# A two-block graph network: beta of the first norm added by ScalarE to the turned tokens

## The reference, cut to what matters

```python
h = jnp.maximum(_layernorm(x, axis=-1), 0.0)
x = x + _L0_gnn_ref(h, adj, ...)      # 8 heads of masked attention, relu
h = jnp.maximum(_layernorm(x, axis=-1), 0.0)
x = x + _L1_gnn_ref(h, adj, ...)      # below
# in _L1_gnn_ref, for each of 3 layers l:
    scores = si[:, :, None] + sj[:, None, :] + attn_b[l]     # then leaky relu, mask
    attn = jax.nn.softmax(scores, axis=-1)
    agg = jnp.einsum('bij,bjd->bid', attn, x)
    h = layernorm(x + agg, g1[l], beta1[l])
    ff = jax.nn.gelu(h @ W1[l] + b1[l], approximate=False) @ W2[l] + b2[l]
    x = layernorm(h + ff, g2[l], beta2[l])
```

## Time and profile before

| | us |
|---|---|
| median of 3 runs | 1536.05 |
| range of the runs | 1535.99 to 1536.13 |
| the profiled execution | 1535.7 |
| its span, first to last instruction | 1533.5 |
| one slot of the second block, most | 25.1 to 25.2 |
| TensorE busy | 1490.6 |
| VectorE busy | 1390.3 |
| ScalarE busy | 1102.2 |
| GpSimd busy | 898.8 |

### The profile page before, as it was taken

One profiled execution on the slowest core, in us unless ns is written; L12 is line 12 of the kernel. 1 busy time (PEld: TensorE's weight loads), 2 busy tenths in 40 slices (PEclk: granted clock), 3 DMA queues, 4 the chain that ended last, 5 costly groups with the idle time before them and its releaser, 6 DMA issues. The chain is left out here.

```text
span 1533.5 us, 35213 instructions
## 1 busy us (share of the span) xinstructions
PE 1490.6 (97%) x11360; PEld 1272.8 (83%) x11360; DVE 1390.3 (91%) x4315; ACT 1102.2 (72%) x1948; POOL 898.8 (59%) x1006
## 2 busy tenths in 40 slices
PE   5899999899999999999999999999999999999997
PEld 3677777778888888888989888988888888888887
DVE  7999999879999999999898999898999998989864
ACT  5788888267777767677777676777777677777774
POOL 5799998336463647463636465645455655455565
PEclk9999999599999999999999999999999999999999
DMA  6643334500000102110001121100011211000001
GB/s 199 167 136 124 134 124 132 169 21 15 8 15 10 47 25 87 35 42 8 15 24 33 38 74 42 36 8 15 25 32 40 71 49 29 8 15 8 15 29 55
DMA packets 70890, 82.79 MB, mean 54 GB/s; under 512 B 29280, under 2 KB 54112, under 8 KB 70752
## 3 DMA queue, kind: packets, MB, share of 16 engines
q1 hardware_dynamic: 69120, 74.76, 16.9%
q0 software_dynamic: 816, 3.15, 0.7%
q10 hardware_dynamic: 816, 3.15, 0.5%
HBM read 38.95 MB, written 25.17 MB: 42 GB/s over the span
## 5 line engine op out<-in xcount | busy, mean ns | idle before, releaser
L874 ACT ACTIVATE bank<-bank,b_col 128x512 f32<-128x512 f32 x384 | 252.0, 656 | 282.9 <-PE bank L773 281.7
L797 PE MATMUL bank<-w_hi,hid_hi 128*128 128x256 f32 x1528 | 433.9, 284 | 6.7 <-DVE hid_lo L1057 6.7
L797 PE MATMUL bank<-w_lo,hid_hi 128*128 128x256 f32 x1528 | 431.8, 283 | 0.0
L797 PE MATMUL bank<-w_hi,hid_lo 128*128 128x256 f32 x1528 | 431.8, 283 | 0.0
L1057 DVE TENSOR_TENSOR hid_lo<-bank,hid_hi 128x512 fp32r<-128x512 f32 x384 | 262.2, 684 | 66.6 <-ACT hid_hi L879 65.3
L773 PE MATMUL bank<-nT_hi,w_hi 128*128 128x512 f32 x768 | 317.3, 413 | 1.2 <-DVE nT_lo L1186 1.2
L797 PEld LDWEIGHTS bank<-w_hi,hid_hi 128*128 128x128 f32 x1528 | 291.2, 191 | 22.9 <-DVE hid_lo L1057 9.7
L773 PE MATMUL bank<-nT_lo,w_hi 128*128 128x512 f32 x768 | 303.4, 395 | 0.0
L773 PE MATMUL bank<-nT_hi,w_lo 128*128 128x512 f32 x768 | 301.9, 393 | 0.0
L797 PEld LDWEIGHTS bank<-w_lo,hid_hi 128*128 128x128 f32 x1528 | 291.5, 191 | 11.8
L797 PEld LDWEIGHTS bank<-w_hi,hid_lo 128*128 128x128 f32 x1528 | 291.4, 191 | 0.0
(11 more groups left out here) (144 smaller groups left out, 3124.5 us busy)
## 6 DMA issues: line engine op xcount, KB each, us to landing
raw_weights<-xin SPq DMA_DIRECT2D x96, 128.0 KB, 2.3
xin<-in_x_dram SPq DMA_DIRECT2D x16, 512.0 KB, 4.0
first_block_out<-x_res SPq DMA_DIRECT2D x16, 512.0 KB, 2.7
second_block_in<-x_act SPq DMA_DIRECT2D x16, 512.0 KB, 3.7
xin<-second_block_in SPq DMA_DIRECT2D x16, 512.0 KB, 3.9
x_fin<-first_block_out SPq DMA_DIRECT2D x16, 512.0 KB, 4.1
out_dram<-x_fin SPq DMA_DIRECT2D x15, 512.0 KB, 2.9
xh_other<-xh SPq DMA_DIRECT2D x128, 33.0 KB, 1.9
```

Of the source, the lines that this page charges most:

```text
L797: mm = pe.matmul(FF[t // 2][:, (t % 2) * D:(t % 2 + 1) * D], a[:, r, t * P:(t + 1) * P], w[:, l, c, :], start=(c == 0 and t % 2 == 0 and p ...
L874: act.activation(h[:], h[:], ACT.Gelu, bias=b1_col[:, l, c:c + 1]).then_inc(s_gelu, 1)
```

## The change

- b1_col is loaded as it is; the splits of beta1, the 96 products and the two additions go. beta1_col stays for the whole kernel.
- ScalarE's `split_n` takes two passes for each half of the tokens: Identity with scale g1 and bias beta1, in place in NT_B, and a rounding copy to nT_hi. The first half is made at chunk 5, the second at chunk 6.
- VectorE's nT_lo is a plain subtraction; its first half comes between low(5) and low(6), its second behind low(7).
- `hidden(0)` waits for each half where it uses it.
- At the start of the second block exp(1,1) comes ahead of gelu(0), VectorE makes scores(0,1) before and dots_of(0,2) behind the first split, TensorE does spread(1,1) ahead of turn_n(0,0), and the first slot has turn_attn and aggregate where the others have them.
- ScalarE's queue issues the loads of W1 at step 3 instead of 2.

```diff
@@ first block, ScalarE
-                    if isinstance(tau, int) and tau == 2:
+                    if isinstance(tau, int) and tau == 3:
                         act.wait_ge(q_ld, 64)
                         for l in range(L):
                             act.dma_start(raw[:, l]...
@@ first block, VectorE
-                    if isinstance(tau, int) and tau == HEAD - 1:
-                        dve.wait_ge(s_col, 48)
-                        dve.tensor_copy(beta1_parts[:, :, :, 0], beta1_col[:]).then_inc(s_beta, 1)
-                        dve.wait_ge(s_beta, 1)
-                        dve.tensor_tensor(beta1_parts[:, :, :, 1], beta1_col[:], beta1_parts[:, :, :, 0].bitcast(F32),
-                                          ALU.subtract).then_inc(s_beta, 1)
@@ TensorE
                 def hidden(U, s, c):
                     l, g = layer_group(s)
-                    if c == 0:
-                        pe.wait_ge(s_nlo, KD * (U + 1))
                     at_least(pe, s_split, CF * U + c - 2)
                     for k in range(KD):
+                        if c == 0:
+                            pe.wait_ge(s_nlo, KD * U + k + 1)
@@
-                def bias(l, cs):
...
                 def tail(tau):
-                    if tau == NT + 5:
-                        bias(0, range(CF))
                     if tau == NT + 6:
                         pe.wait_ge(s_samer, 1)
                         pe.wait_ge(q_ev, NT)
                         spread(0, 0)
-                        bias(1, range(CF // 2))
-                    if tau == NT + 7:
-                        bias(1, range(CF // 2, CF))
                     if tau == NT + 8:
                         turn_attn(0, 0)
                     if tau == NT + 9:
                         pe.wait_ge(q_vh, 2 * NT)
                         aggregate(0, 0)
-                        bias(2, range(CF))
                 def before():
+                    spread(1, 1)
                     turn_n(0, 0)
-                    spread(1, 1)
@@ (in some)
-                            if nxt and c == (1 if U == 0 else 0):
+                            if nxt and c == 0:
                                 turn_attn(U + 1, s + 1)
-                            if nxt and c == (2 if U == 0 else 1):
+                            if nxt and c == 1:
                                 aggregate(U + 1, s + 1)
@@ ScalarE
-                def split_n(V, s):
+                def split_n(V, s, ks=range(KD)):
                     l, g = layer_group(s)
-                    for k in range(KD):
+                    for k in ks:
                         act.wait_ge(s_nT, KD * V + k + 1)
-                        act.activation(nT_hi[:, s % 2, k, :], NT_B[k][:], ACT.Copy, scale=g1_col[:, l, k:k + 1]).then_inc(s_nhi, 1)
+                        act.activation(NT_B[k][:], NT_B[k][:], ACT.Identity, bias=beta1_col[:, l, k:k + 1],
+                                       scale=g1_col[:, l, k:k + 1]).then_inc(s_nfull, 1)
+                        act.wait_ge(s_nfull, KD * V + k + 1)
+                        act.copy(nT_hi[:, s % 2, k, :], NT_B[k][:]).then_inc(s_nhi, 1)
@@ (before)
                     split_n(0, 0)
-                    act.wait_ge(s_b1, 2)
+                    exp(1, 1)
@@ (in some)
-                            if nxt and c == (1 if U == 0 else 0):
+                            if nxt and c == 0:
                                 keep_attn(U + 1, s + 1)
                             high(U, s, c)
-                            if U == 0 and c == 0:
-                                exp(1, 1)
...
-                            if nxt and c == 5:
-                                split_n(U + 1, s + 1)
+                            if nxt and c in (5, 6):
+                                split_n(U + 1, s + 1, (c - 5,))
@@ VectorE (split_n)
                         dve.wait_ge(s_nhi, KD * V + k + 1)
-                        dve.scalar_tensor_tensor(nT_lo[:, s % 2, k, :], NT_B[k][:], g1_col[:, l, k:k + 1],
-                                                 nT_hi[:, s % 2, k, :].bitcast(F32), ALU.mult, ALU.subtract).then_inc(s_nlo, 1)
+                        dve.tensor_tensor(nT_lo[:, s % 2, k, :], NT_B[k][:], nT_hi[:, s % 2, k, :].bitcast(F32),
+                                          ALU.subtract).then_inc(s_nlo, 1)
@@ (before)
-                    dots_of(0, 2, range(0, 2))
-                    dve.wait_ge(s_bias, L)
...
+                    scores(0, 1)
                     first_part_over(dve)
                     split_n(0, 0)
-                    scores(0, 1)
+                    dots_of(0, 2, range(0, 2))
@@ (in some)
                         low(U, s, 5)
                         if nxt:
-                            split_n(U + 1, s + 1)
+                            split_n(U + 1, s + 1, (0,))
                         low(U, s, 6)
                         if nxt3:
                             dots_of(i, s + 3, range(0, 1))
                         low(U, s, 7)
+                        if nxt:
+                            split_n(U + 1, s + 1, (1,))
```

32 lines of the change are left out of this document (6 added, 26 removed).

## The result

The changed kernel takes 1514.56 us (median of 4 runs, 1514.12 to 1515.4), the kernel before 1536.02 us in the same set: ratio 0.9861, 95% interval 0.9844 to 0.9878, faster by 1.4%. Executions of the kernel before fall in two groups, 1533.3 to 1535.0 and 1536.2 to 1536.7 us in the set that has most of them, and the four of this set lie near the upper one. The profiled execution took 1515.0 us, its span 1513.2 us, 20.3 us less than before.

What follows compares the result with a forecast made beforehand. TensorE, busy for 97% of the span, bounds the kernel, VectorE the slots with a mask. 1.4 + 0.7 + 7.0 + 6.3 = 15.4 us off 1535.7 gives 1520.3, with 0.35 for the median 1520.6; range 1515 to 1527.5.

Steps and rivals of the forecast that it cites:

- first block: Before the second block: W1 loads issued a step later win 1.4 us, the split of beta leaving VectorE 0.7.
- hand-over: Start of second block: fewer bias products, earlier hidden(0), two table loads gone; 7.9 us less 0.9 given back, 7.0.
- mask slots: The 12 slots where VectorE also makes a mask: low(7) starts 1.2 us earlier, 6.3 us won of 7.5 lost.
- So in 35 slots nothing changes.: Second-block slots without a mask: VectorE's moved half only lengthens idle time or is covered, so no gain.
- I take 1.4: First block: hT(0) and hrelu(1) run before the W1 loads; VectorE 1.9 us earlier, then 1.6; bounds 0.3 and 1.9.
- The 0.7 for the split of beta: First block, step 15: VectorE's two instructions, 0.37 and 0.53 us less overlap, go; bounds 0.3 and 0.9.
- the three waits: VectorE's waits for TensorE before the first norm_n, 1.12, 1.25 and 1.61 us, behind bias products: 3.6 us won.
- the 0.9 that a held mask was to give back: Hand-over: make_mask(0,2) meets GpSimd's first base and is held, about 0.9 us lost.
- VectorE as the bound of the mask slots: Rival, chance 0.20: the dot products stay held in the 12 slots, 3.2 us or less won; 1523.8 to 1527.
- The clock rival: Rival, chance 0.10: hand-over gives 5 us or less, as the clock stays low or mask and base collide; 1522.6 to 1526.
- The slower rival: Rival, chance 0.04: ScalarE's new pass late for gelu(7) in 47 slots; 0.33 us beyond 0.9 covered eats the gain.
- The signs: Profile after: hid_lo waits gone but slot 0, first hidden matmul some 6 us earlier, hidden(3) some 9, src_hi at 14.8.

Runs made afterwards that it cites:

- the order alone: The kernel before with only VectorE's second nT_lo moved behind low(7) and TensorE waiting for each half by itself: 1525.57 us, ratio 0.9932.
- the extra wait: The changed kernel with one more, long fulfilled wait on ScalarE between exp(1,1) and the first gelu: 1514.05 us.
- the run with 128 bytes: The changed kernel with 128 bytes a partition left free behind beta1_col: 1509.05 us in a single execution, beside 1536.40 of the kernel before.
- the run with two more copies: The changed kernel with the rounding copy of the second nT_hi done three times, the visit 1.24 us longer: 1535.3 us, ratio 0.9999.

## Why the prediction was right or wrong

| part | forecast | bounds | found (us of the span, one trace of each kernel) |
|---|---|---|---|
| first block | 2.1 | 0.6 to 2.8 | 0.2 |
| hand-over | 7.0 | 5.2 to 8.4 | 7.0 |
| mask slots | 6.3 | 3.2 to 7.5 | 8.2 |
| other slots | 0 | none | 2.2 |
| places of the tiles | not seen | none | 2.8 |
| sum | 15.4 | | 20.4, measured 20.3 |

**The step that failed** is "So in 35 slots nothing changes." It rested on an empty list of waits. The starts of turn_n, 25.12 and 25.24 us apart by turns, said that something was lost in every second slot, and hid_lo(7) at 740.80 beside output(7) at 740.85 said where. The run with the order alone gives 2.2 us for these slots. The same oversight set the upper bound of the mask slots: 7.5 us is the loss against an ordinary stretch, taken as TensorE's own pace of 25.2 us a slot, and that pace had losses of its own. Against 25.12 the loss is 8.2, and all of it was won. The term of the mask slots is a right mechanism of a wrong size, 6.3 for 8.2: low(7) came 1.07 us earlier (forecast 1.2), and the dot products in front of it stayed held, 1.39 us.

**The places** are a gain of 2.8 us that no row of before could tell, and no part of what the change is about. The time lies 0.44 us below the range, so each of the two unforeseen gains, this one and the 2.2 us of the ordinary slots, was enough to put it there: with the tiles at their old places the changed kernel takes 1517.09 us, inside the range. Shown is that 64 bytes of padding take it back; why TensorE's matmuls of 256 columns take 280 instead of 282 ns with one place and not with another stays open.

**The first block** was over-sized. By the table over eighteen traces the two steps together are worth 0.8 us, for 2.1, within the bounds of 0.6 to 2.8; the pair in the table above has 0.2. "I take 1.4" held for some us: the lead is 1.7 at VectorE's first src_hi and 1.1 at the third no_edge. The forecast let TensorE do its part at the pace of the trace of before, but with the work moved forward, in the changed kernel's trace though not in all, more of it falls in the slow time: the score products took 0.78, 0.63 and 0.58 us where they had taken 0.49, 0.38 and 0.38. The 0.7 for the split of beta was not found: in that pair VectorE's lead is 0.1 us more behind the step than in front of it.

**The hand-over** came out right as a sum, and partly by luck. Up to hidden(0) the chain was right: the three waits were worth 3.5 us at turn_n(0) (forecast 3.6), and hidden(0) started at 299.79 (forecast 299.7, without the 0.2 of lead). From there to hidden(3) it took 9.79 us where the forecast has 9.1, since hidden(1) ran at the low clock to 305.60, and the forecast goes on from 304.9. Against that the 0.9 that a held mask was to give back did not reach TensorE: hidden(3) to turn_n(1) is 8.68 us, before 8.81. The two errors cancel.

What made the later part shorter is only in part shown. With exp(1,1) and its two loads put back turn_n(1) comes some 0.8 us later, and the medians differ by 0.4, less than the forecast gave them. The load of the gelu's table, which the forecast kept on the path, left it; the extra wait put it back, and that cost nothing in this kernel. And the clock of 0.71 over 312 to 317 us before, where hidden(2) and output(0) ran, was 1.00 in the same work after. But it was 1.00 in the trace of the order alone too, where TensorE still waits 1.88 us for attn in place of 2.27. So the two table loads are not what that clock hangs on alone. The edits put back one at a time, 1.7 and 0.4 us in the medians and 2.9 and 0.8 at turn_n(1), don't add up to 7.0; the rest comes from several of them together, and was not taken apart.

**The rivals.** VectorE as the bound of the mask slots did not happen, but would at once with a faster TensorE, as the run with 128 bytes suggests (its mask slots 25.05 to 25.23 us beside ordinary ones near 24.90, six waits for hid_lo, one execution). The clock rival was half right: it stays low through hidden(1), and mending it is worth 2.1 to 2.9 us. The slower rival named the right point, a visit of 2.5 us at chunk 6 that takes the whole gain, and the run with two more copies measured that; but a loss of 0.33 us a slot was to eat a gain of 15.4, and it was 0.42 that ate one of 20, so the agreement is partly luck. The table was loaded no more often: 46 times at the exp and 47 at the gelu.

**The signs.** TensorE's one wait for hid_lo is left in slot 0, as forecast. The first hidden matmul came 3.8 us earlier, not some 6, and hidden(3) 7.1, not some 9, mostly because the first block gave so little; VectorE's src_hi came at 15.29 in this trace (forecast 14.8).

With 0.2, 7.0, 8.2 + 2.2 and 2.8 in place of its terms the sum would have given 1535.7 + 0.35 - 20.4 = 1515.7 us, within the range; the last 1.1 us lie outside the spans (0.4) and in the median of the changed kernel, 0.4 below its profiled execution and not 0.35 above it. The 0.44 us are smaller than that. The range ended too high because its bounds were made from recorded waits alone.

## What to carry to other kernels

An empty list of waits doesn't say that an engine runs at its own pace: take the period of the loop from the starts of one instruction in many rounds, and ask of every difference, even of 0.1 us, what ends just before the late start. A piece of work should be moved out of the front of a just-late producer only as far as the idle time that it fills allows: one nT_lo behind low(7) won 10.3 us in the slots, two dot products behind it lost 3.4 (1170.55 against 1167.20 us from turn_n(1) to turn_n(47)). And when two versions differ by 0.1 or 0.2% in a kernel that waits for nothing, shift the tiles by some bytes before believing in a cause. Nor does one trace of each kernel tell a few tenths of a us in a start-up or a hand-over: the same code differed by 1 to 2 us there from trace to trace.

## What the runs showed of the hardware

- The pace of TensorE depends on where tiles lie in a partition. Slots of the same instructions took 25.12, 25.06, 25.04, near 24.90 (one execution) and 25.06 us with hid_hi at byte 207776, 207712, 207808, 207840 and 207968 (the tiles of the second block all move with it). Between the ends lie 7.8 us (1156.87 and 1149.07 from turn_n(1) to turn_n(47)), over a third of what the whole change won.
- A wait of some 0.1 us before a matmul shows in no list and in no idle time; 46 waits listed as 7.0 us cost 18.7.
- In the first 20 us the rows show a granted clock of 1.00, but TensorE did four products in 2.02 to 2.18 us that take 1.08 later; with 13 matmuls in front of them they took 1.18.
- A wait that was long fulfilled moved a table load of 1.28 us from ahead of another wait to behind it.
- Keeping TensorE busy with unread matmuls in its idle time at the hand-over made the kernel faster by 2.1 to 2.9 us; at the start it won nothing.
- Where TensorE's rate rises behind an idle stretch differs between executions: in eight traces with the same hand-over turn_n(0) to turn_n(1) took 20.86 to 22.27 us.
